# Steady lists of TensorE, ScalarE, VectorE and GpSimd in another order, with the value products in adjacent pairs

## What is computed

```
h = layernorm(x) * (1 + ca) + sa
x = x + ga * attention(h)      # rmsnorm, 16 heads of 64, causal softmax, a sigmoid gate per head, output matrix
h = layernorm(x) * (1 + cb) + sb
x = x + gb * ffn(h)            # silu(h Wg + bg) * (h Wu + bu) @ Wd + bd, plus product-key experts
```

## Time and profile before

| what | value |
|---|---|
| median of 3 runs | 1448.64 us |
| profiled execution, from first to last instruction | 1448.7 us |
| PE busy | 1399.7 us, 97% |
| VectorE busy | 1289.4 us, 89% |
| ScalarE busy | 1270.9 us, 88% |
| GpSimd busy | 1052.9 us, 73% |
| DMA | 27.74 MB, mean 19 GB/s |

### The profile page before, as it was taken

One profiled execution on the slowest core, in us unless ns is written; L12 is line 12 of the kernel. 1 busy time (PEld: TensorE's weight loads), 2 busy tenths in 40 slices (PEclk: granted clock), 3 DMA queues, 4 the chain that ended last, 5 costly groups with the idle time before them and its releaser, 6 DMA issues.

```text
span 1448.7 us, 39838 instructions
## 1 busy us (share of the span) xinstructions
PE 1399.7 (97%) x11491; PEld 1161.5 (80%) x11491; DVE 1289.4 (89%) x5345; ACT 1270.9 (88%) x4212; POOL 1052.9 (73%) x1221
## 2 busy tenths in 40 slices
PE   6899999999999999999999999999999999999998
PEld 4678788888788888788888788888788888788887
DVE  5589999999999999999999999999999999999977
ACT  6788988898988898988898988898988898988885
POOL 2048787778787777787777787787787777777760
PEclk9999999999999999999999999999999999999999
DMA  4000000000000000000000000000000000000000
GB/s 132 16 14 21 15 10 20 20 16 20 13 11 20 20 16 20 14 10 20 20 16 20 13 11 20 20 16 20 15 9 20 20 16 20 14 10 24 10 14 10
DMA packets 51041, 27.74 MB, mean 19 GB/s; under 512 B 10336, under 2 KB 50208, under 8 KB 51008
## 3 DMA queue, kind: packets, MB, share of 16 engines
q1 hardware_dynamic: 50768, 26.91, 7.1%
q10 hardware_dynamic: 240, 0.43, 0.1%
HBM read 23.02 MB, written 4.31 MB: 19 GB/s over the span
## 4 chain that ended last, share of the span: by engine, by line
PE 81%; ACT 14%; issue 3%; DVE 1%; DMA 0%; SPq 0%; POOL 0%; ACTq 0%; DVEq 0%; POOLq 0%
PE pW L1457 10%; PE pS L1527 9%; PE pW L1540 9%; PE pW L1568 8%; PE pW L1459 8%; PE pW L1458 8%; PE pS L1517 7%; PE pS L1513 6%; PE pW L1613 4%; PE pW L1610 4%; ACT pT L652 4%; ACT pS L660 4%; PE pW L1544 3%; PE pW L1601 2%; ACT h L750 2%
## 5 line engine op out<-in xcount | busy, mean ns | idle before, releaser
L660 ACT ACTIVATE pS<-pS,nmx 128x128 f32<-128x128 f32 (+1 forms) x1024 | 389.4, 433 | 33.2 <-DVE nmx L1085 33.2
L1085 DVE CUSTOM_DVE_ANT_0 pS<-pS,mask 128x128 f32<-128x128 f32 (+1 forms) x1024 | 331.8, 390 | 27.2 <-PE pS L1517 22.7
L504 POOL TENSOR_TENSOR fexp<-fexp,fsum 128x512 f32<-128x512 f32 x240 | 299.9, 1284 | 76.6 <-DVE fexp L1214 76.6
L652 ACT COPY pT<-pS 128x768 f32<-128x768 f32 x256 | 216.1, 844 | 42.2 <-PE pS L1527 40.4
L495 POOL TENSOR_TENSOR fsum<-ex 128x512 f32<-128x512 f32 x248 | 250.6, 1047 | 0.0
L1527 PE MATMUL pS<-ident,p_sb 128*128 128x128 f32 x1536 | 216.3, 277 | 6.1 <-DVE p_sb L1105 4.2
L1105 DVE TENSOR_TENSOR p_sb<-pS,coef 128x256 f32<-128x256 f32 (+2 forms) x512 | 210.5, 453 | 8.9
L1527 PEld LDWEIGHTS pS<-ident,p_sb 128*128 128x128 f32 x1536 | 173.7, 141 | 37.3 <-issue 18.9
L660 ACT ACTIVATION_READ_ACCUMULATOR pS<-pS,nmx 128x1 f32 x1024 | 193.7, 189 | 0.0
L642 ACT COPY qk<-pW 128x512 f32<-128x512 f32 x256 | 162.2, 634 | 4.6 <-PE pW L1459 1.1
L1540 PE MATMUL pW<-pT,v 128*64 128x256 f32 x1024 | 165.9, 402 | 0.3 <-ACT pT L652 0.2
(11 more groups left out here) (211 smaller groups left out, 3696.1 us busy)
## 6 DMA issues: line engine op xcount, KB each, us to landing
x_in<-in_L_attn_tokens SPq DMA_DIRECT2D x32, 128.0 KB, 2.1
x_res<-in_L_attn_tokens SPq DMA_DIRECT2D x32, 128.0 KB, 3.0
modB<-mods_dram SPq DMA_DIRECT2D x32, 128.0 KB, 2.9
modA<-mods_dram SPq DMA_DIRECT2D x31, 128.0 KB, 3.1
out<-yo SPq DMA_DIRECT2D x31, 128.0 KB, 1.9
modC<-mods_dram SPq DMA_DIRECT2D x32, 64.0 KB, 3.2
fsum<-in_L_attn_Wkv SPq DMA_DIRECT2D x1, 512.0 KB, 6.0
w_out<-in_L_attn_Wout SPq DMA_DIRECT2D x1, 512.0 KB, 7.2
```

Of the source, the lines that this page charges most:

```text
L504: ins = nc.gpsimd.tensor_tensor(fexp[:, k, h, :], fexp[:, k, h, :], fsum[:, k, h].rearrange("p i j -> p (i j)"), ALU.mult)
L652: nc.scalar.copy(pT[:, p % 2], pS[:, p % 2, :, 0:SW]).then_inc(S(pT_ready), 1)
L660: ins = nc.scalar.activation(ps, ps, ACT.Exp, bias=nmx[:, p % 2, h, k:k + 1], scale=-1.0, accum_out=den(p)[:, h, k:k + 1])
L1085: ins = nc.vector.tensor_tensor_reduce(out=ps, in0=ps, in1=mask[:, (1 - k) * P:2 * P], scale=-1.0, scalar=LARGEST, op0=ALU.add, op1=ALU.mi ...
```

## The change

Four things are in the diff. The steady lists of the four engines have another order; on PE, `weigh_values` now always comes in adjacent pairs (6 and 7, 0 and 1, 2 and 3, 4 and 5). The bank table follows the new filling order. A semaphore `ex_ready` is added, by which GpSimd waits in `products(k)` for ScalarE's `expert_exp(k)`, and `gate_up(0)` of ScalarE also waits for bank `y` to be full. In iteration 0 `project_v(1)` and `weigh_values(2)` stand a little later. No operation is added to or taken from an iteration's arithmetic.

```diff
+        ex_ready = [ev(f"ex{k}_ready", 1) for k in range(TB)]
...
-        order = [("V", 0, 0), ("QK", 2, 0), ("QK", 3, 0), ("V", 3, 0), ("PV", 6, -1), ("GU", 1, -2),
...
+        order = [("QK", 2, 0), ("V", 0, 0), ("QK", 3, 0), ("V", 3, 0), ("D", 0, -2), ("PV", 6, -1), ("PV", 7, -1),
...
                 def products(k):
                     if w.live(-2):
+                        pool.wait_ge(S(ex_ready[k]), at(ex_ready[k], g, 1))
...
+                products(0)
                 candidates()
-                products(0)
+                add_bias()
                 products(1)
+                rstd1()
                 weigh(0)
-                add_bias()
                 add_heads(0)
+                rstd2()
                 fold(0)
-                rstd2()
                 weigh(1)
-                rstd1()
                 add_heads(1)
                 rms1()
                 fold(1)
...
+                        if c == 0 and w.has("y") and not (isinstance(i, int) and i == B):
+                            w.wait_full("y")
...
                 thresholds()
+                choose(0, 0)
                 row_max(0)
-                choose(0, 0)
                 choose(0, 1)
+                ln1_stats()
                 row_max(1)
...
+                normalise(3)
                 choose(1, 1)
-                normalise(3)
-                ln1_stats()
                 bias_product(3)
                 gate_product(3)
+                ln1_modulate()
                 row_max(4)
...
-                ln1_modulate()
                 shift(1)
...
+                project_down(0)
                 scores(1)
                 weigh_values(6)
+                weigh_values(7)
                 gate_up(1)
-                weigh_values(7)
-                project_down(0)
-                project_v(1)
+                gate_up(2)
...
```

More of the change, by code:

```diff
@@ L790, in body @@
                     scale_head(1)
-                    values(1)
                     copy_transposes(0, 0)
@@ L804, in body @@
                     queries(5)
+                    values(1)
                     exp_scores(4)
+                    values(2)
                     weighted(2)
-                    values(2)
                     queries(6)
@@ L869, in body @@
                     return
+                values(0)
                 copy_transposes(7, -1)
                 queries(2)
-                values(0)
                 queries(3)
+                values(3)
                 exp_scores(0)
+                down_tanh(0)
                 weighted(6)
-                values(3)
+                weighted(7)
+                exp_scores(1)
                 gate_up(1)
-                exp_scores(1)
-                weighted(7)
-                down_tanh(0)
                 scale_head(1)
+                gate_up(2)
                 copy_transposes(0, 0)
+                copy_transposes(1, 0)
+                queries(4)
                 down_tanh(1)
-                copy_transposes(1, 0)
-                gate_up(2)
-                values(1)
[L889 to L893, removed]
-                weighted(1)
[L895 to L900, removed]
+                exp_scores(2)
+                queries(5)
+                exp_scores(3)
+                gate_up(3)
+                total(0)
+                scale_head(3)
+                weighted(0)
+                copy_transposes(2, 0)
+                values(1)
+                rows2()
+                copy_transposes(3, 0)
+                weighted(1)
+                values(2)
+                modulate_h()
+                queries(6)
                 values(4)
-                modulate_h()
                 high_part(h2T_high, h2T, "hT")
                 exp_scores(4)
-                queries(6)
                 weighted(2)
-                values(2)
+                weighted(3)
                 exp_scores(5)
+                scale_head(5)
                 queries(7)
-                values(5)
-                scale_head(5)
-                weighted(3)
                 copy_transposes(4, 0)
@@ L915, in body @@
                 total(1)
+                experts(0)
+                values(5)
+                rms_scale()
                 weighted(4)
                 expert_exp(0)
[L918 to L921, removed]
                 weighted(5)
                 experts(1)
+                high_part(xT_high, xT, "xT")
                 exp_scores(6)
+                expert_exp(1)
                 exp_scores(7)
@@ L1479, in project_qk @@
                             pe.wait_ge(qkv_low, 1 if i < 0 else 3)
+                        if isinstance(i, int) and i == 1 and p == 2:
+                            pe.wait_ge(su_act, 5)
                         w.wait_free("QK", p)
@@ L1493, in project_v @@
                                 pe.wait_ge(su_act, 4)
-                        if isinstance(i, int) and i == 1 and n == 0:
-                            pe.wait_ge(su_act, 5)
                         w.wait_free("V", n)
@@ L1813, in body @@
                 project_out()
+                gate_up(3)
+                project_v(1)
+                transpose_scores(2, 0)
                 weigh_values(0)
                 weigh_values(1)
-                transpose_scores(2, 0)
-                project_qk(4)
-                gate_up(3)
-                project_qk(5)
-                project_v(4)
                 transpose_scores(3, 0)
                 scores(4)
+                project_v(2)
                 transpose_h()
+                project_qk(6)
+                project_v(4)
                 scores(5)
                 weigh_values(2)
-                project_qk(6)
-                project_v(2)
+                weigh_values(3)
+                project_qk(7)
                 similarity(0)
                 project_v(5)
-                project_qk(7)
-                weigh_values(3)
+                similarity(1)
                 transpose_scores(4, 0)
-                similarity(1)
                 transpose_scores(5, 0)
                 transpose_experts(0)
+                scores(6)
+                scores(7)
                 weigh_values(4)
                 weigh_values(5)
-                scores(6)
-                scores(7)
+                transpose_experts(1)
                 transpose_x()
-                transpose_experts(1)
+                gate_up(0)
                 project_ffn(0)
                 project_ffn(1)
-                gate_up(0)
+                transpose_scores(6, 0)
                 project_qk(0)
-                transpose_scores(6, 0)
                 project_qk(1)
```

36 lines of the change are left out of this document (19 added, 17 removed), and 10 rows, old and new, of the table order.

## The result

The kernel after takes 1643.85 us (median of 4 runs, 1642.75 to 1648.5) against 1448.32 us before (4 runs, 1445.79 to 1448.77): ratio 1.136, 95% interval 1.134 to 1.137. The forecast was 1605, with a range of 1490 to 1660. The profiled execution spans 1641.0 us.

What follows compares the result with a forecast made beforehand. PE bounds the kernel, with VectorE 3.7 us from it; VectorE would take over with 46.4 us busy plus 2.5 idle, 48.85 us against 43.44. Over 29 iterations that adds 157 us to 1448.7: 1605 us, range 1490 to 1660.

Steps and rivals of the forecast that it cites:

- The deciding term: VectorE's `ln1_modulate` beside large GpSimd instructions: five to six instructions held, 5.4 us more per iteration.
- The upper bound: At `ln1_modulate`, all six instructions each wait for a whole L504 of 1.24 us: 7 us.
- The smaller ones: Further VectorE holds by GpSimd: `choose(0, 0)` +0.7 us, `choose(1, 0)` +0.5 us per iteration; `top_d` stays held.
- VectorE above 93% busy: Sign expected in the new profile if the forecast is right, together with PE below 90%.
- The idle term: VectorE idle time per iteration: 0.9 us remaining, 0.7 at `normalise(5)`, 0.9 at `bias_product(0)`; 2.5 us.
- up to 1.5 us: Possible half-clock delay of PE's last 10 us before `finish`, per iteration; up to 44 us, only in the range.
- the long wait of PE: PE idle about 5 us in a row at the first `transpose_scores` behind `ln1_modulate`.
- The pairs: Adjacent value products on PE: two broken pairs fewer, about 0.3 us each, 0.6 us less per iteration.
- rival 1: VectorE and GpSimd do not hold each other at `ln1_modulate`, pairs win on PE: 1422 us (1410 to 1430); chance 0.08.
- Rival 1 and 2: No holding; the second adds `fold(0)` delaying GpSimd's `weigh(1)`, 1443 us (1435 to 1450), chance 0.08.
- rival 3: GpSimd falls behind, one to three `ln1_modulate` instructions held: 2 us per iteration, 1507 us (1460 to 1560); chance 0.14.

Runs made afterwards that it cites:

- e1: Kernel after, with `ln1_modulate` alone moved back behind `shift(0)` on VectorE: 1561.8 us, ratio 1.077.
- e3: Kernel after, with GpSimd's `weigh(1)` and the first two sums of `add_heads(1)` on 32 of 512 elements: 1482.1 us, ratio 1.023.
- e8: Kernel before, with `ln1_modulate` moved up behind `gate_product(3)` and its producers `ln1_stats` and `rstd1` moved up too: 1676.7 us, ratio 1.157.
- e6: Kernel after's PE and ScalarE lists and bank table, with VectorE and GpSimd in nearly the order of before: 1602.5 us, ratio 1.106.
- e11: Kernel after, with `weigh_values(2)` done six times over to keep PE at work in its hole: 1599.1 us, ratio 1.104.
- e4: Kernel before, with value products 6, 7 and 2, 3 paired on PE, ScalarE and bank table following, VectorE and GpSimd untouched: 1499.0 us, ratio 1.034.
- e7: Kernel before, with only pair 6, 7 closed by a later `gate_up(1)`, new bank table, `exp_scores(1)` and `normalise(1)` ahead of the gates: 1478.0 us, ratio 1.020.
- e9: Kernel before, with the engine orders of e7 but the bank table of before: 1481.7 us, ratio 1.023.
- e13: As e12, with `weigh_values(2)` also moved back directly ahead of `weigh_values(3)`, bank table and ScalarE's copies following: 1469.3 us, ratio 1.014.
- e12: Kernel before, with `gate_up(1)` moved ahead of `weigh_values(6)` so pair 6, 7 closes, ScalarE following, bank table unchanged: 1445.1 us, ratio 0.9975.
- e2: Kernel before, with `ln1_modulate` alone moved up behind `gate_product(3)`, ahead of its producer `rstd1`: 1725.0 us, ratio 1.190.

## Why the prediction was right, and where it was not

**The deciding term.** `ln1_modulate` meets GpSimd's `fold(0)` and `weigh(1)`: forecast five to six instructions held by 0.98 us, 5.4 us together. Measured are five, held by 0.80, 0.98, 0.97, 0.95 and 0.94 us (medians less the unheld medians), 4.6 us. e1 and e3 show cause and price from both sides, by the place and by GpSimd's length; e8 shows that this step, with its producers, is enough. They don't make it the whole loss: e1 gives back 82 of the 195 us and e6 41, with no instruction of the block held in either, since PE meets another long wait in both; e3, which keeps every list, gives back 162. The rule that the prediction quotes from the Trainium skill, page SBUF — State Buffer, section Who interferes with whom, spoke against the change, and it did hold for these lines: the trace agrees, with 1.14 to 1.39 us each (medians) for five of the six. The upper bound, a whole L504 each, was not reached.

**The smaller ones.** `choose` was forecast at +1.2 us together, 0.7 at `choose(0, 0)` and 0.5 at `choose(1, 0)`. Its group in the page (busy us, mean ns, idle before):

```profile
L1218 DVE TENSOR_SCALAR fexp<-fsum,top,rz 128x512 f32<-128x512 f32 x240 | 185.9, 815 | 1.1
```

Before, the mean was 675 ns; (815 - 675) x 8 per iteration = +1.1 us. The sum fits by luck: by their places in the list, `choose(0, 0)` has both halves held (medians 1.08 and 1.26 us, before 0.55 and 0.54), +1.25 us, and `choose(1, 0)` has one half held as before, which is -0.1. `top_d` I expected still to be held; it is free now (281 ns in place of 1341), 1.06 us less. Together 4.6 + 1.1 - 1.1 = 4.7 us more busy VectorE, against 4.8 in the windows. I had 6.6. This term was 1.9 too large, and with it the forecast of VectorE above 93% busy was wrong: it is 89% in the steady stretch (1247.20 / 1399.31), PE also 89%, as forecast below 90%.

**The idle term.** This is the step of the sum that was furthest off: 2.5 us forecast, 49.98 - 44.5 = 5.4 measured. Summed over the steady stretch, VectorE's idle time per iteration is 2.2 us at `low_part` of `xT` (the second wait of the list above), 1.4 in hand-overs too short for the list, 0.7 at `normalise(5)`, 0.7 at `finish` for PE's `project_ffn`, and the rest small. Of what I had listed, `normalise(5)` came as priced (0.7); the hand-overs were 1.4 in place of 0.9; `bias_product(0)`, priced at 0.9, doesn't wait at all (0.01); `finish` and `low_part` I had at nothing.

The 2.2 us are mostly the half clock. I left it out of the sum and had it only in the range, as "up to 1.5 us"; no row stood behind that figure. In e11, where the clock stays full, that one wait is 0.3 us, VectorE's idle time 3.0 us, and an iteration 48.3 us, where my sum, made without the half clock, says 48.85; the run of that case is at 1599 us where the forecast is 1605. Part of that nearness is luck again: in e11 `top_d` is held (median 1.12 us), so that VectorE is busy for 45.3 of the 48.3 us (1313.20 / 1400 of the window above). That is 94%, the "above 93%" of the forecast.

The place was wrong too. I had the long wait of PE at the first `transpose_scores` behind the block, and it is at `weigh_values(3)`, for a bank, 4.0 us. The length (about 5) was near, the released thing was not. PE also waits 1.1 us per iteration at `gate_up(2)`, where I did not look; e1 and e11 have the same wait, and no run takes it away.

**So** 1605 was 2.4% low: the error of an iteration, 49.98 - 48.85 = 1.13 us, times 29 is 33 us, and the rest lies outside the steady stretch. An overpriced busy term (1.9 us) hid about as much as the half clock cost (1.7), which was luck; the mechanism, five instructions held one after another, was not.

**The pairs.** Three of the four pairs have their value products 0.70 us apart in the kernel after, as forecast. The fourth, 2 and 3, does not: in every steady iteration the hole of 4.0 us lies inside it, and its products are 4.9 us apart. So half of the 0.6 us is not even there, and the rest doesn't reach the end, since PE is not the bound. That PE alone could have turned them into a gain was the basis of rival 1, and e4, e7, e9 and e13 show it false in four arrangements: each frees some bank or hands over some operand later, and an iteration is 0.6 to 1.7 us longer than before. The one arrangement that gains (e12) gains half of what I priced for a pair, for the price is paid per change of kind between neighbours, and `scores` is such a change anyway.

**The rivals.** Rival 1 and 2 (nothing is held) and rival 3 (one to three held) are refuted by the lines above. `fold(0)` ahead of `weigh(1)` is in fact one of the instructions that hold. What remains open is how the 195 us divide between the held instructions and the waits that the new lists of PE and ScalarE bring by themselves (e1 and e6 lose 114 and 154 us without a held instruction in the block).

## What to carry to other kernels

A step of VectorE whose operands lie in SBUF has a price that depends on what GpSimd runs beside it: count its instructions, not its time, and price each at up to one GpSimd instruction (here +0.8 to +1.0 us beside ones of 1.24 us); place such a step where GpSimd waits, best for that step itself. When a hole opens in PE, here of 2.3 us or more, look at the granted clock behind it, and put what it costs (here 1.6 to 1.7 us per iteration) into the sum, not into the range. Before two products are made neighbours, ask whose bank the one between them holds and how soon it is wanted; moving `gate_up(1)` earlier gained here (e12), moving it later lost in all three runs (e4, e7, e9).

## What the runs showed of the hardware that was not expected

In the kernel after the half clock comes once per iteration, behind each hole of 4 us, and does not last equally long. Windows like those above, two iterations later, where PE starts again at 829.71:

```profile
829.00:832.40 3.40, 2.69 (x13) 1.98 (x14) 3.25 (x15) 2.96 (x15) 3.24 (x5) 0.54 0.00 0
832.40:835.80 3.40, 3.40 (x12) 2.92 (x11) 2.56 (x14) 1.96 (x8) 0.35 (x1) 0.50 0.00 0
```

That is at least 6.5 us at 1.2 GHz ((0.46 + 0.50) / 0.5 x 3.4) behind the same hole that gave 3.4 us above, and the iteration is 50.7 us in place of 49.3. In the kernel before, whose PE is never idle for more than 0.5 us in the steady stretch, it is absent, and so it is in e11, with up to 1.15 us. In e8, with a hole of up to 5.9 us, the mean granted clock is 0.94, in e2 with up to 7.4 us 0.93. Holes of 2.3 us are enough, but not every time: the clock falls behind them in 23 of 28 iterations of e1 and in 6 of 28 of e6. No run shows what decides it. Filling a hole with useless products of PE is worth 45 us here.

The two engines take turns, one instruction each: from 721.67 to 728.38 us GpSimd's L526 and four L506 and VectorE's five held instructions end alternately. The last L1007 is not held: it begins at 728.31 us, between the last L506 and the first L513, and it is L513 that takes 0.15 us longer than the second one.

A held instruction shows as a long duration and not as idle time or as a wait: neither the list of waits nor the idle columns name the cause anywhere in the kernel after. What finds it is the shortest duration of a line beside its median.
